# Mamba stage: the next group's preparation placed anew among the 64 steps, with fewer scaled tiles on VectorE

## The reference

```python
xn = x * jax.lax.rsqrt(jnp.mean(x * x, axis=-1, keepdims=True) + EPS) * g
xz = xn @ W_in.T
x_s, z = jnp.split(xz, 2, axis=-1)
# xc: causal convolution of x_s over 4 positions, then silu
params = xc @ W_x.T                      # B (16), C (16), log_dt (1)
dt = jax.nn.softplus(log_dt @ W_dt.T + b_dt)
A_bar = jnp.exp(dt_e * A)                # 512 features x 16 states
Bu = dt_e * B_coef[:, :, None, :] * xc[..., None]
# scan over positions: h = A_bar * h + Bu;  y = sum over states of h * C
y = (y + xc * D) * jax.nn.silu(z)
return residual + y @ W_out.T
```

## Time and profile before

| | us |
|---|---|
| median of 3 runs (3852.84 to 3854.54) | 3854.36 |
| the profiled execution | 3851.82 |
| its span, from the first to the last instruction | 3850.0 |
| first scan of the Mamba stage starts at | 1281.0 |
| last scan of the Mamba stage starts at | 3085.6 |

### The profile page before, as it was taken

The page is one execution under the profiler, slowest core; times in us unless marked ns, Lnnn a source line. Parts: engine busy times, 40 slices in busy tenths (PEclk is TensorE's granted clock), DMA queues, the critical chain, the costliest instruction groups (busy, mean ns, idle before and its releaser), DMA issues. The chain is left out here.

```text
span 3850.0 us, 75338 instructions
## 1 busy us (share of the span) xinstructions
PE 3303.3 (86%) x23328; PEld 2503.5 (65%) x23360; DVE 3137.9 (82%) x5227; ACT 2770.0 (72%) x5061; POOL 2650.3 (69%) x2987
## 2 busy tenths in 40 slices
PE   8996988979964688888888888888898869997887
PEld 5664666667442467677767667767676757775565
DVE  5665899955395798999898989999899949998887
ACT  2223787844475888888888888888888837776887
POOL 1222677730095799999898998999998936665676
PEclk9997999979976899999999999999999989998999
DMA  2111122251112111111111111111111112322121
GB/s 65 54 54 54 42 52 53 50 114 38 44 44 73 43 50 55 56 47 55 48 51 55 56 49 51 51 51 57 55 48 50 53 43 63 78 55 66 50 61 44
DMA packets 285550, 209.63 MB, mean 54 GB/s; under 512 B 131416, under 2 KB 249752, under 8 KB 285224
## 3 DMA queue, kind: packets, MB, share of 16 engines
q1 hardware_dynamic: 285224, 205.72, 19.7%
HBM read 149.18 MB, written 51.41 MB: 52 GB/s over the span
## 5 line engine op out<-in xcount | busy, mean ns | idle before, releaser
L2896 POOL TENSOR_TENSOR ma_ch<-ma_h,ma_crep 128x512 f32<-128x512 f32 x1024 | 1371.0, 1361 | 161.2 <-DVE ma_h L2998 148.0
L2998 DVE TENSOR_TENSOR_SCAN ma_h<-ma_a,ma_pbu 128x512 f32<-128x512 f32 x1024 | 1212.4, 1206 | 174.8 <-PE ma_pbu L2576 113.9
L2576 PE MATMUL ma_pbu<-ma_ident,ma_bu 128*128 128x128 f32 x4096 | 659.9, 285 | 199.2 <-DVE ma_h L2998 158.9
L2576 PEld LDWEIGHTS ma_pbu<-ma_ident,ma_bu 128*128 128x128 f32 x4096 | 480.0, 144 | 441.9 <-DVE ma_h L2998 313.6
L2783 ACT ACTIVATE ma_a<-ma_dt,ma_A 128x510 f32<-128x510 f32 x1024 | 653.2, 717 | 2.0 <-issue 2.0
L2585 PE MATMUL ma_py<-ma_ident,ma_ch 128*128 128x128 f32 x4096 | 627.5, 279 | 0.8 <-POOL ma_ch L2896 0.8
L2774 ACT ACTIVATE ma_bu<-ma_uT,ma_b_t 128x512 f32<-128x512 f32 x784 | 508.0, 718 | 17.1 <-PE ma_pbu L2576 15.3
L2585 PEld LDWEIGHTS ma_py<-ma_ident,ma_ch 128*128 128x128 f32 x4096 | 498.2, 146 | 1.3 <-POOL ma_ch L2896 1.3
L1576 POOL TENSOR_TENSOR xa_prob<-xa_e,xa_rec_head 128x616 f32<-128x616 f32 x128 | 155.7, 1218 | 125.7 <-DVE xa_rec_head L1668 113.6
L924 POOL TENSOR_TENSOR xa_prob<-xa_e,xa_rec_head 128x616 f32<-128x616 f32 x128 | 155.7, 1217 | 108.0 <-DVE xa_rec_head L1016 89.5
L362 POOL TENSOR_TENSOR la_veps<-la_mv,la_eps 128x2 f32<-128x2 f32 x32 | 6.3, 197 | 249.6 <-DVE la_mv L395 249.6
(11 more groups left out here) (375 smaller groups left out, 8007.3 us busy)
## 6 DMA issues: line engine op xcount, KB each, us to landing
ma_crep<-ma_ct_dram SPq DMA_DIRECT2D x256, 256.0 KB
xa_x<-act SPq DMA_DIRECT2D x64, 256.0 KB, 2.8
act<-xa_y SPq DMA_DIRECT2D x64, 256.0 KB, 2.2
la_x<-in_x SPq DMA_DIRECT2D x32, 256.0 KB, 2.8
act<-la_y SPq DMA_DIRECT2D x32, 256.0 KB
act<-ea_x SPq DMA_DIRECT2D x32, 256.0 KB, 4.0
ma_x<-act SPq DMA_DIRECT2D x16, 512.0 KB, 4.6
ma_xr<-act SPq DMA_DIRECT2D x16, 512.0 KB
```

The lines of the kernel that those rows point to most:

```text
L2576: last = pe.transpose(pbu[c % 2][:, t * P:(t + 1) * P], bu[:, s % 2, t, c * P:(c + 1) * P], ident[:, :])
L2896: pool.tensor_tensor(ch[:, s % 2, c], h[:, s % 2, c], crep[:, s % 4, :], ALU.mult).then_inc(multiplied, 1)
L2998: dve.tensor_tensor_scan(out=h[:, s % 2, c, :], data0=a[:, s % 2, c, :], data1=pbu[c % 2][:, :], initial=0.0, op0=ALU.mult, op1=ALU.add).t ...
```

## The change

Four things change, all in `mamba`:

1. ACT's `group` walks ten places q per state s: `decay` of c stands at q = 2c, `scale_b(s + 1)` at q = 8, and each other operation at its own (s, q). `squares` becomes `square_of`, one tile a time.
2. PE, DVE and POOL get tables (s, c) for the same operations as before, at other places.
3. `DVE_TILES` names 3 tiles a group instead of 7, `POOL_TILES` 7 instead of 8; ACT makes the other 54 (49 before). POOL's tiles are made one to two states earlier (`TILE_AT`), behind `times_c` of that step.
4. POOL scales a tile by `tensor_scalar` with the column as scalar operand, times 1.0, where it was a `tensor_tensor` with the column broadcast.

```diff
-        DVE_TILES = {1: 1, 7: 2, 8: 1, 9: 1, 10: 1, 15: 1}
-        POOL_TILES = {2: 1, 3: 1, 4: 1, 5: 1, 6: 1, 9: 1, 10: 1, 11: 1}
+        DVE_TILES = {9: 1, 10: 2}
+        POOL_TILES = {2: 1, 3: 1, 4: 1, 5: 1, 6: 1, 7: 1, 10: 1}
...
-            GATED = {(2, 2): 0, (2, 3): 1, (3, 1): 2, (3, 2): 3}
...
-            PARAMETERS = {(6, 2): 0, (6, 3): 1, (7, 0): 2, (7, 1): 3}
...
-            U = {(13, 3): 0, (14, 0): 1, (14, 3): 2, (15, 0): 3}
+            TURN_X = {(0, 2): 0, (1, 1): 1}
+            X0 = {(1, 2): 0, (2, 3): 1, (3, 3): 2, (4, 3): 3}
+            X1 = {(1, 3): 0, (2, 3): 1, (3, 3): 2, (4, 3): 3}
+            SKIP = {(12, 0): 0, (10, 1): 1, (11, 3): 2, (12, 1): 3}
+            SPREAD_L = {(8, 0): 0}
+            TURN_B = {(12, 3): 0}
+            GATED = {(2, 1): 0, (2, 3): 1, (3, 1): 2, (3, 2): 3}
+            OUT = {(4, 1): (0, 0), (4, 2): (0, 1), (5, 0): (1, 0), (5, 3): (1, 1), (8, 2): (2, 0), (9, 1): (2, 1), (9, 2): (3, 0), (9, 3): (3, 1)}
+            PARAMETERS = {(6, 0): 0, (6, 1): 1, (7, 1): 2, (7, 2): 3}
+            Z = {(12, 1): (0, 0), (12, 2): (0, 1), (13, 0): (1, 0), (13, 1): (1, 1), (13, 2): (2, 0), (13, 3): (2, 1), (14, 0): (3, 0), (14, 1): (3, 1)}
+            U = {(13, 0): 0, (13, 3): 1, (14, 2): 2, (15, 0): 3}
...
-                        if (s, c) == (7, 2) and prep:
+                        if (s, c) in SPREAD_L and prep:
                             spread_l(n)
-                        if (s, c) == (9, 2) and prep:
+                        if (s, c) in TURN_B and prep:
                             turn_b(n)
...
+            TAP = {(2, 6): 0, (3, 6): 1, (4, 8): 2, (6, 1): 3}
+            XT = {(1, 2): 0, (1, 7): 1}
+            SQUARES = {(2, 5): 0, (3, 0): 1, (3, 1): 2, (5, 1): 3}
+            YV = {(3, 5): 0, (3, 6): 1, (3, 9): 2, (4, 2): 3}
+            SILU = {(6, 7): 0}
+            COPY_P = {(8, 4): 0}
+            SIZE = {(9, 1): 0, (9, 4): 1}
+            EXP = {(9, 6): 0, (10, 3): 1}
+            COPY_B = {(13, 5): 0}
+            LOG = {(10, 3): 0, (11, 9): 1}
+            COPY_Z = {(13, 3): 0, (13, 8): 1, (14, 6): 2, (15, 6): 3}
+            COPY_U = {(13, 9): 0, (14, 9): 1, (15, 4): 2, (15, 7): 3}
...
-                pool.tensor_tensor(bu[:, s % 2, t, :], uT[:, par, t, :],
-                                   b_t[:, par, t, s:s + 1].broadcast_to([P, DI]), ALU.mult).then_inc(pool_tile_ready, 1)
+                pool.tensor_scalar(bu[:, s % 2, t, :], uT[:, par, t, :], b_t[:, par, t, s:s + 1], 1.0,
+                                   ALU.mult, ALU.mult).then_inc(pool_tile_ready, 1)
...
-            INPUTS = {(11, 1): 0, (11, 3): 1, (12, 1): 2, (12, 3): 3}
+            INPUTS = {(11, 3): 0, (12, 3): 1, (13, 1): 2, (13, 2): 3}
+            RSTD = {(6, 1): 0, (11, 0): 1}
+            RMS = {(4, 1): 0}
+            DIAGONAL = {(7, 3): 0}
+            TILE_AT = {(0, 3): 2, (3, 0): 4, (8, 3): 10, (1, 3): 3, (4, 0): 5, (5, 3): 7, (5, 0): 6}
...
-            STATS = {(5, 2): 0, (5, 3): 1, (10, 0): 2, (10, 1): 3}
-            INPUTS = {(13, 0): 0, (13, 1): 1, (13, 3): 2, (14, 0): 3}
-            FINISH = {(7, 0): 0, (7, 1): 1, (11, 2): 2, (11, 3): 3}
+            GATE = {(1, 2): 0, (2, 0): 2}
+            CONV1 = {(2, 2): 0, (3, 1): 1, (4, 2): 2, (5, 1): 3}
+            CONV2 = {(2, 2): 0, (3, 2): 1, (4, 2): 2, (5, 1): 3}
+            CONV3 = {(2, 2): 0, (3, 2): 1, (4, 2): 2, (5, 2): 3}
+            VAR = {(6, 2): 0, (11, 1): 1}
+            ONE = {(10, 0): 0, (10, 3): 1}
+            LOST = {(10, 2): 0, (13, 0): 1}
+            TAKE = {(11, 2): 0, (12, 2): 1, (13, 1): 2, (14, 0): 3}
+            STATS = {(6, 0): 0, (6, 1): 1, (10, 0): 2, (10, 2): 3}
+            INPUTS = {(12, 3): 0, (13, 2): 1, (14, 0): 2, (14, 3): 3}
+            FINISH = {(7, 1): 0, (7, 2): 1, (12, 0): 2, (12, 1): 3}
```

More of the change, by code:

```diff
@@ L2645, in group @@
                                 done += 1
[L2646 to L2650, removed]
+                        if (s, c) in TURN_X and prep:
+                            turn_x(n, TURN_X[s, c])
+                        if (s, c) in X0 and prep:
+                            project_x(n, X0[s, c], 0)
+                        if (s, c) in X1 and prep:
+                            project_x(n, X1[s, c], 1)
                         if (s, c) in GATED and not first:
@@ L2706, in copy_z, with square_of @@
                 act.activation(sz[:, par, t, :], src[:, :], ACT.Copy).then_inc(z_copied, 1)
-            def squares(n, tiles):
+            def square_of(n, t):
                 act.wait_ge(x_loaded, 16 * n + 16)
-                for t in tiles:
-                    act.activation(square[:, t, :], x[:, t, :], ACT.Square, accum_out=ssq[:, t:t + 1]).then_inc(ssq_ready, 1)
+                act.activation(square[:, t, :], x[:, t, :], ACT.Square, accum_out=ssq[:, t:t + 1]).then_inc(ssq_ready, 1)
             def copy_xT(n, c):
@@ L2792, in group @@
                 for s in range(N):
-                    if s != 6:
-                        decay(g, par, s)
-                    if 2 <= s < 2 + IC and prep:
-                        first_tap(n, np_, s - 2)
-                    if s == 1 and prep:
-                        for c in range(C):
-                            copy_xT(n, c)
-                    if s in SQUARES and ahead:
-                        squares(g + 2, SQUARES[s])
-                    if s in (3, 4) and not first:
-                        copy_gated(g - 1, 2 * s - 5)
@@ L2817, in group @@
-                    if s == 15 and prep:
-                        copy_uT(n, np_, 2)
-                        copy_uT(n, np_, 3)
-                    if s + 1 < N:
-                        scale_b(g, par, s + 1)
-                    elif prep:
-                        scale_b(n, np_, 0)
-                    if s in (2, 3) and not first:
-                        copy_gated(g - 1, 2 * (s - 2))
-                    if s == 5:
-                        decay(g, par, 6)
-                        silu_z(g, par)
-                        if prep:
-                            silu_x(n, np_)
-                        act.preload_act_table_set("natural_log_exp_and_others")
@@ L2846, in _ @@
             link(act.activation(A[:, :, :], A[:, :, :], ACT.Copy, scale=-1.0))
-            squares(0, range(TT))
+            for t in range(TT):
+                square_of(0, t)
             act.wait_ge(setup_done, 1)
@@ L2866, in _ @@
                 step_log(0, half)
-            squares(1, range(TT))
+            for t in range(TT):
+                square_of(1, t)
             for c in range(IC):
@@ L2896, in times_c, with tile_may_be_scaled @@
                 pool.tensor_tensor(ch[:, s % 2, c], h[:, s % 2, c], crep[:, s % 4, :], ALU.mult).then_inc(multiplied, 1)
-            def scale_tile(g, par, s):
+            def tile_may_be_scaled(g, s):
                 pool.wait_ge(uT_copied, IC * g + IC)
```

126 lines of the change are left out of this document (69 added, 57 removed).

## The result

| | before | after |
|---|---|---|
| median, us (4 runs each) | 3853.6 (3852.77 to 3854.54) | 3800.49 (3790.86 to 3802.73) |
| the profiled execution, and its span | 3851.82, 3850.0 | 3800.63, 3797.8 |
| first and last scan of the stage start at | 1281.0, 3085.6 | 1277.5, 3027.8 |

The ratio is 0.9863, 95% interval 0.9848 to 0.9879: 53 us less. Forecast were 3793, within 3752 to 3852. In this result and in the experiments one single execution, of e10, was in a slow state; it lasted 6194 us and is in no ratio. First the groups of instructions of the changed kernel (group | busy us, mean ns | idle time before them and who ended it), and one line, GpSimd's tile, by itself (ns min/median/max).

The account below looks back on a forecast made before the run. Four engines, 85 to 91% busy, were taken to hold each other up. Seven parts of a group summed to -4.05 us, -61 over 15 groups; 3851.8 less 61 plus 2.5 gave 3793 us, range 3752 to 3852.

Parts of the forecast that it names:

- Part D: Steps (5,2) to (8,1) of a group: idles around scan (8,0) and three DVE tiles go, 20.0 to 15.9 us.
- The sum: All seven parts of a group added: -4.05 us, over 15 groups that prepare a next one -61 us.
- Part E: Steps (8,1) to (10,0): scans, two tiles, statistics, `one_plus` and PE wait take 10.9 us instead of 12.2.
- Parts F and G: Steps (10,0) to (13,0), +0.9 us, and on to the next group, +0.6: operations moved in, POOL contention.
- rival 1: POOL binds from step (10,0) to the group's end, its dt additions nearer their use: 3824 us, chance 0.20.
- Parts A and B: Steps (0,0) to (2,2), +0.6 us, tap behind x's load; to (3,0), +0.9, gated tile's copy late.
- Part C: Steps (3,0) to (5,2): less idle behind projections and one statistics moved out, 18.6 us instead of 20.3.
- The tile: POOL's tile with a scalar operand takes 0.8 us instead of 1.09, bounds 478 to 956 ns.
- Rival 2: Steps (0,0) to (3,0) lose nothing, taps and gates in time: 3770 us, down to 3755, chance 0.12.
- rival 3: ACT, with five more tiles, becomes the bound: a group takes +1.1 us, 3871 us in all, chance 0.14.
- Rival 4: The new places only shift the idle, each one gone replaced: within 8 us of 3854, chance 0.06.

Follow-up runs that it names:

- e10: The changed kernel with three places corrected (parameters, first square, fourth statistics), and one piece of `project_out` moved from (8,2) to (9,0): 3766.95 us, ratio 0.9777.
- e8: The changed kernel with VectorE's fourth statistics of the gated tile moved from step (10,2) to (10,1): 3782.22 us, ratio 0.9832.
- e1: The kernel before with GpSimd's tiles scaled by `tensor_scalar` and its waits for a tile ahead of `times_c`: 3849.51 us, ratio 0.9992.
- e2: The kernel before with the new tile numbers and GpSimd's scalar form, at the old places: 3852.14 us, ratio 0.9996.
- e3: The changed kernel with the old tile numbers, old GpSimd form and old tile steps, so the new places alone: 3816.97 us, ratio 0.9902.

## Why the prediction was right, and where it was off

**Part D (forecast -4.1, measured -3.1).** The mechanism was right and carries the result: no wait of scan (8,0) for ACT, and PE waiting at (6,0) for silu (0.81 and 0.62 us of idle, against 1.3 forecast). Two terms of the sum were missing. The statistics that C gave away (0.33) were never added to D. And the products at (7,1) and (7,2) cost 0.52 us in front of (7,3), which had been taken as covered. The forecast window of 15 to 17 held.

**The sum.** Fifteen groups at -4.05 were to give 61 us. The fifteen that prepare a next group gave 47.8 (14 times 3.25, and 2.3), which is 13 less, and the last group gave 6.6 for which the sum had no term. That 53 came so near to 61 is luck to that extent.

**Part E (forecast -1.3, measured +0.2).** This is the step that failed. I costed `one_plus` at its own 0.6 and gave a wait for GpSimd only to the tiles; it took 1.79 and the tiles 0.74 and 1.04. Where E had 0.8 us of idle behind `project_out`, the profile has 0.71.

**Parts F and G (forecast +0.9 and +0.6, measured -0.6 and +1.2).** "0.5 us of wait for each" turn is a mean over places that each cost between nothing and 1.1 us, the same in group after group, set by the order in which the engines start. Over E, F and G together the forecast was +0.2 and the outcome +0.8: as a mean it was usable, for one place it was not. e8 shows that such a term can be placed. In G there was another loss too, and it is rival 1's: the dt addition of GpSimd came late, and DVE waited 1.27 us for it ahead of scan (13,2) in seven of the groups (before: once in the stage, 1.3 us).

```profile
L3001 DVE TENSOR_TENSOR ma_av<-ma_dt,ma_xc 128x512 f32<-128x512 f32 x60 | 79.8, 1329 | 9.2 <-POOL ma_dt L2910 8.9
```

These 8.9 us are 0.6 a group, the size of G's miss.

**Parts A and B (forecast +0.6 and +0.9, measured 0.0 and +0.5).** The wait for x ahead of the tap came, but with 2.01 us and not the 3 that I named: x landed 13.4 us into the group and not 14.0, and the tap ran at 14.4. DVE waited 1.20 for the tap in group 8. And I had forgotten in A that a tile of VectorE left it: the first step of the group fell from 1.87 to 1.32 us on average. Scan (3,0) waits 1.55 us for PE in group 8, as forecast.

**Part C (forecast -1.65, measured -1.5)** held.

**The tile** on GpSimd takes 0.70 us, below my 0.8 and the 0.75 to 0.9 I named. It bought nothing by itself (e1), so the forecast's band for this cost was wider than it had to be. GpSimd's idle rose to 190.5, where I had it fall to about 100: a sign that I named and that failed. I had charged the whole of DVE's turns to GpSimd as well; its `times_c`, 1361 ns on average before, take 1340 after, so it pays for fewer turns than before and not for more.

**The rivals.** GpSimd did not bind F and G (rival 1): DVE waited 2.1 us for it before scans, and the misses that the rival names came about once in two groups and not three times in each. Rival 2 came true by half: A lost nothing, B lost 0.5. ACT did not become the bound (rival 3): its wait at the parameters fell by 2.7 us and its whole idle time in the stage from 260.7 to 160.3, 6.7 a group where I forecast 7; e2 shows what would have come without that. Rival 4 fails by C and D, 4.6 us together. From the rule cited under rival 3, in the Trainium skill (VectorE: DVE Perf Modes, the perf-mode tier table), that an f32 `tensor_scalar` in SBUF runs in the 2x mode, I took VectorE as the cheap place for a tile. In the old places the measurement stands neither for nor against that (e2, 0.9996). In the new places four tiles fewer on VectorE and GpSimd's new form, numbers and steps together took the ratio from 0.9902 to 0.9863. Which of these gave it wasn't tried, so this is not shown to be VectorE's tiles; what the traces show is their price beside a busy GpSimd, 0.81 us on average in the changed kernel and up to 3.68 in e3, against 0.46 alone.

## What to carry to other kernels

When four engines are each busy for 85 to 90% of a stage, look for the one wait that ends last in each stretch and move what stands in front of it; one reordering gave 45 us here, while a faster instruction and a better division of tiles gave nothing in the old order. Count the first and the last turn of a loop by themselves: here the last group did other work, had another bound and gave 6.6 us that no sum over the others could show. Then test the new order piece by piece: an operation that waits for a load, put in front of one that others wait for, cost 7 to 14 us, and one that starts just behind the other engine's instruction cost 12 to 18. An idle that is taken away is worth only what the next operation behind it doesn't lose.
